# A kernel of three stages on one core: loads and copies of the first pair reordered, the last stage's interleaving rewritten, one VectorE turn split in two

## The chip, the cores and the metric

One core of a Trainium2 chip. The time is that of one execution in microseconds of device time, the median of three runs. A profile of one execution comes with it.

## The reference

Eight samples of 64 rows of width 512 (f32) pass three layers, each added to its input. 

```python
x = x + xattn(layernorm(x), ctx, ctx)   # 1 head: softmax(q k^T / sqrt(512)) v over 1601 context rows
x = x + attn(layernorm(x))              # 16 heads of 32, 64 rows: per head
#   q, k normalised per head; resonance = sigmoid((q k^T - 0.29514) * 15)
#   modulation = resonance * gate_q[:, None] * gate_k[None, :];  out = (modulation @ v) @ Wo + bo
x = x + ffn(layernorm(x))
#   sel = argmax(x @ gate_w.T) of 8 experts, rw = sigmoid(max);  xs = x * rw
#   out = ((xs @ w_up[sel].T) * silu(xs @ w_gate[sel].T)) @ w_down[sel].T
```

## The kernel before, in words

**Pairs.** The eight samples are worked on as four pairs (128 rows each, `p` = 0 to 3). A pair first has its cross attention: *scores* against 1601 keys in 13 units (`score(p, u)`; four units for each of three chunks of 512 keys and one for the last 65), then *sums* (the numerators are turned, `turn_numerators`, copied by ScalarE or VectorE, `move_numerators`, and multiplied with the context, `weigh`). The self attention of pair p-1, its norms and its choice of experts (`attention(p - 1, step)`, step names as in `STEPS`) are laid between the units of pair p by hand. Pairs 1 and 2 are one hardware loop, pair 3 is written out.

**Keys.** Scores need the context with its width on the partitions. For pair 0 some chunks are turned by TensorE (`FIRST.turns`) and copied out of PSUM by ScalarE and VectorE (`move_keys`). All others are loaded into `FF_sb` in pieces of 512 B (`load_split`) and turned in blocks of 32x32 by VectorE (`turn_split(p, ch, c)`, line 874, read at `CT_sb<-FF_sb`). Part 2 of pair p's split load (the third chunk, turned as `turn_split(p, 2, c)`, c = 0 to 3) can only be issued when `turn_split(p, 1, 3)` has freed its slots. `turn_split(p, 2, 0)` is what score unit 4 waits for, `turn_split(p, 2, 3)` is what unit 7 waits for.

**Queues.** SyncE issues nearly all loads in one fixed order, ScalarE issues the upper halves of pair 1's split loads (`upper_first`). GpSimd issues the gathers and scatters of rows (indirect DMAs: `get`, `put`) and does the powers (`pow`) of the norms.

**The ending.** The self attention of the last pair (`_L` = 3) is interleaved with the expert stage, whose rows lie in tiles: four wide ones (0 to 3) and two narrow ones (4 and 5, in a loop over rounds, here one). A tile f has the steps get (gather), xT (turn the rows), up0 to up3 (gate and up product, each a quarter of the depth), act (ScalarE's tanh, then two VectorE instructions), hT (turn), down (product; VectorE adds it to the rows). One table, `ENDING`, then `LATE`, is walked by every engine in order; an engine does what a step holds for it. So a step's place sets what it waits behind on each engine.

## Time and profile before

| | us |
|---|---|
| median of three runs | 330.53 (329.59 to 330.92) |
| the profiled execution's own time | 324.69 |
| its span, first to last instruction | 323.0 |
| TensorE busy | 294.6 (91%), granted clock 0.975 of full speed |
| VectorE, ScalarE, GpSimd busy | 165.2, 87.9, 79.4 |
| the DMA engines, page's slices | nine tenths or more until about two thirds of the span, 240 GB/s on average |

TensorE is the engine to read first; idle times of the others count only where TensorE waits for them. Times of views are from the span's start.

### The profile page before, as it was taken

How to read it: one execution, taken by the hardware profiler on the slowest of the kernel's cores; microseconds unless marked ns; L12 is line 12 of the kernel's file. 1: busy time of each engine (PE TensorE's matmuls, PEld its weight loads, DVE VectorE, ACT ScalarE, POOL GpSimd, SP SyncE). 2: the span in 40 equal slices, each digit the busy share in tenths (PEclk: the TensorE clock that was granted, in tenths of full speed). 3: DMA queues.
4: the chain of work that ended last, by engine and by line, in shares of the span. 5: the costliest groups of instructions: out<-in, count | busy, mean ns of one | idle time of the engine just before them, and what ended most of it. 6: DMA issues, size and time to landing. Idle time of an engine off the chain costs nothing. (4 is left out here: it accounts for less than half of the span.)

```text
span 323.0 us, 4958 instructions
## 1 busy us (share of the span) xinstructions
PE 294.6 (91%) x1628; PEld 143.3 (44%) x1628; DVE 165.2 (51%) x381; ACT 87.9 (27%) x209; POOL 79.4 (25%) x87
## 2 busy tenths in 40 slices
...
GB/s 238 375 296 286 231 315 318 289 232 275 227 386 200 213 270 223 168 306 386 234 229 338 81 207 380 309 298 360 90 67 179 422 411 225 42 213 78 143 13 36
DMA packets 67541, 77.41 MB, mean 240 GB/s; under 512 B 3220, under 2 KB 46260, under 8 KB 66497
## 3 DMA queue, kind: packets, MB, share of 16 engines
...
HBM read 74.00 MB, written 3.67 MB: 240 GB/s over the span
## 5 line engine op out<-in xcount | busy, mean ns | idle before, releaser
L874 DVE STREAM_TRANSPOSE CT_sb<-FF_sb 128x1024 f32<-128x1024 f32 (+1 forms) x56 | 50.7, 952 | 22.0 <-DMA FF_sb<-ctx 20.8
L1385 PE MATMUL ST<-CTX_sb,PR_sb 128*64 128x512 f32 (+1 forms) x208 | 48.2, 600 | 1.1 <-ACT PR_sb L361 1.1
L1347 PE MATMUL SC<-CT_sb,QC_sb 128*64 128x512 f32 x112 | 29.8, 650 | 4.9 <-DVE CT_sb L874 4.9
L1230 PE MATMUL A<-AW_sb,normT_sb 128*128 128x512 f32 x64 | 29.5, 604 | 0.1
L1385 PEld LDWEIGHTS ST<-CTX_sb,PR_sb 128*64 128x64 f32 (+1 forms) x208 | 13.9, 136 | 23.2 <-issue 22.3
L1230 PEld LDWEIGHTS A<-AW_sb,normT_sb 128*128 128x128 f32 x64 | 11.5, 189 | 15.7 <-issue 11.9
L1253 PE MATMUL A<-AW_sb,WQK_sb 128*128 128x256 f32 x64 | 15.9, 412 | 1.5 <-DMA WQK_sb<-wq 1.5
L546 POOL TENSOR_TENSOR rn_sb<-ss_sb,nhalf_sb 128x16 f32<-128x16 f32 x4 | 11.7, 2917 | 22.3 <-DVE ss_sb L948 22.3
L575 POOL TENSOR_TENSOR sq_sb<-AW_sb,rowv_sb 128x512 f32<-128x512 f32 x4 | 5.1, 1273 | 45.9 <-DMA AW_sb<-awk 35.2
L1347 PEld LDWEIGHTS SC<-CT_sb,QC_sb 128*64 128x64 f32 x112 | 7.3, 144 | 20.2 <-issue 11.0
L1230 PE MATMUL A<-AO_sb,rawT_sb 128*128 128x512 f32 x32 | 14.8, 605 | 1.2 <-DVE rawT_sb L987 1.2
L1327 PE MATMUL SC<-CT_sb,QC_sb 128*64 128x256 f32 x112 | 15.7, 418 | 0.0
L1253 PEld LDWEIGHTS A<-AW_sb,WQK_sb 128*128 128x128 f32 x64 | 13.1, 208 | 3.9 <-DMA WQK_sb<-wq 1.8
L1230 PE MATMUL A<-WV_sb,rawT_sb 128*128 128x512 f32 x32 | 14.7, 602 | 0.0
L693 ACT COPY QC_sb<-QK_sb 32x128 f32 (+1 forms) x48 | 14.2, 296 | 1.1
L1286 PE MATMUL A<-AO_sb,WQK_sb 128*128 128x128 f32 (+1 forms) x64 | 14.5, 382 | 0.0
L714 ACT COPY rawT_sb<-A 128x512 f32<-128x512 f32 x4 | 2.3, 586 | 42.8 <-PE A L1223 34.3
L549 POOL TENSOR_TENSOR rn_sb<-ss_sb,nhalf_sb 128x16 f32<-128x16 f32 x4 | 11.6, 2903 | 6.8 <-DVE ss_sb L955 6.8
L540 POOL TENSOR_TENSOR rstd_sb<-rstd_sb,halves_sb 128x3 f32<-128x3 f32 x4 | 3.5, 877 | 39.2 <-DVE rstd_sb L933 39.2
L558 POOL TENSOR_TENSOR rstd_sb<-rstd_sb,nhalf_sb 128x1 f32<-128x1 f32 x4 | 2.2, 562 | 39.5 <-DVE rstd_sb L995 39.5
L701 ACT ACTIVATE PR_sb<-SC,mx_sb 128x512 f32<-128x512 f32 x12 | 8.1, 684 | 12.9 <-DVE mx_sb L898 12.9
L889 DVE TENSOR_REDUCE mx_sb<-SC 128x1 f32<-128x512 f32 x12 | 8.2, 681 | 6.4 <-PE SC L1327 6.3
...
## 6 DMA issues: line engine op xcount, KB each, us to landing
...
FF_sb<-ctx SPq DMA_DIRECT2D x48, 256.0 KB, 6.9
...
FF_sb<-ctx ACTq DMA_DIRECT2D x8, 256.0 KB, 12.1
...
```

The source lines that it names most:

```text
L546: g.tensor_tensor(rn[:, 0:HEADS], ss[:, 0:HEADS], nhalf[:, 0:HEADS], ALU.pow).then_inc(s["powq"], 1)
L549: g.tensor_tensor(rn[:, HEADS:], ss[:, HEADS:], nhalf[:, HEADS:], ALU.pow).then_inc(s["powk"], 1)
L693: a.copy(qcurP[m * Q:(m + 1) * Q, j, :], qk[j * Q:(j + 1) * Q, m, bass.ds(p * P, P)]).then_inc(s["qcurP_made"], 1)
L701: a.activation(prow[:, keys], chunk_scores[c], ACT.Exp, bias=mx[:, NCH + 2:NCH + 3], scale=scale, accum_out=esum[:, c:c + 1]).then_inc(s[" ...
L874: v.transpose(ring[:, c, :, to:to + n * Q].rearrange("p k (b r) -> p k b r", r=Q), split[:, :, at:at + n, c * Q:(c + 1) * Q]).then_inc(s[" ...
L889: link(v.tensor_reduce(mx[:, c:c + 1], chunk_scores[c], AX.X, ALU.max))
L1230: last = t_.matmul(bank, left[:, c, :], right[:, c, :], start=(c == 0), stop=(c == DC - 1))
L1253: last = t_.matmul(AB[m % 2][:, 0:2 * P], wq[:, c, m * P:(m + 1) * P], xnT[:, c, 2 * P * half:2 * P * (half + 1)], start=(c == 0), stop=(c ...
L1286: last = t_.matmul(AB[m % 2][:, n], wkT[:, c, m * P:(m + 1) * P], qpT[:, c, n], start=(c == 0), stop=(c == DC - 1))
L1327: last = t_.matmul(SC[q, at:at + GT * P], queries(p, own)[:, i, q], ring[:, i, k, at:at + GT * P], start=(i == 0), stop=(i == DC - 1))
L1347: last = t_.matmul(SC[q, ch * D:(ch + 1) * D], queries(p, own)[:, c, q], ring[:, c, k, :], start=(c == 0), stop=(c == DC - 1))
L1385: last = t_.matmul(ST[q, :], probs[0:w, t, q], ctxb[0:w, k, t, :], start=(t == 0), stop=(t == KT - 1))
```

## The change

Seven edits: (1) SyncE loads `awq`, `awk` and `wv` later in the first pair; (2) ScalarE copies its last turned keys and a bias row before it issues split loads; (3) VectorE turns pair 1's second chunk ahead of a copy of numerators and of two sums; (4) `turn_split(p, 2, 3)` is done as two halves, by sample, around the normalising of the rows; (5) the tables `ENDING` and `LATE` are reordered, with three wide tiles instead of two stored late; (6) VectorE's five counting instructions stand after `choose(_L)`; (7) the count of stores is taken per queue signal.

```diff
-ENDING = (... (0, "xT"), (_L, "on"), (1, "xT"), (_L, "y"), (0, "up0"), (0, "up1"), (0, "up2"), (0, "up3"),
...
+ENDING = ((0, "get"), (1, "get"), (_L, "sum"), (0, "xT"), (_L, "on"), (_L, "y"), (0, "up0"), (0, "up1"), (0, "up2"), (0, "up3"),
+          (_L, "stats"), (_L, "norm"), (2, "get"), (3, "get"), (_L, "a2"), (0, "act"), (1, "xT"), (_L, "q"), (_L, "graw"), (0, "hT"),
+          (_L, "k"), (_L, "fold"), (_L, "v"), (_L, "kT"), (_L, "turn"), (1, "up0"), (1, "up1"), (_L, "align0"), (_L, "align1"),
+          (0, "down"), (_L, "bd"), (_L, "gT"), (_L, "col"), (2, "xT"), (_L, "o"), (1, "up2"), (_L, "hnorm"), (_L, "h"), (1, "up3"),
+          (_L, "route"), (2, "up0"), (2, "up1"), (_L, "rank"), (2, "up2"))
+LATE = ((1, "act"), (2, "up3"), (1, "hT"), (3, "xT"), (2, "act"), (1, "down"), (3, "up0"), (2, "hT"), (3, "up1"), (3, "up2"),
+        (2, "down"), (3, "up3"), (3, "act"), (3, "hT"), (3, "down"))
-LATE_WIDE = (2, 3)
+LATE_WIDE = (1, 2, 3)
...
             sp.wait_ge(s["qp_made"], 2 * DC)
-            load_weight(awq, "awq", "aq_in")
-            load_weight(awk, "awk", "ak_in")
             load_chunk(0, 1)
             sp.wait_ge(s["keysT_made"], split_turned(0, FIRST.keys(1, 3)))
             load_split(sp, 1, 0, LOWER)
-            load_weight(wv, "wv", "wv_in")
+            load_weight(awq, "awq", "aq_in")
+            load_weight(awk, "awk", "ak_in")
             sp.wait_ge(s["keysT_made"], split_turned(0, FIRST.keys(0, 3)))
             load_split(sp, 1, 1, LOWER)
+            load_weight(wv, "wv", "wv_in")
             load_weight(awv, "awv", "av_in")
...
-            for turn in FIRST.turns[2:6]:
+            for turn in FIRST.turns[2:5]:
+                move_keys(act, a.copy, 0, 0, turn)
+            act.wait_ge(s["c_made"], 1)
+            a.copy(crow, AB[1][:, :]).then_inc(s["c_moved"], 1)
+            for turn in FIRST.turns[5:]:
                 move_keys(act, a.copy, 0, 0, turn)
             upper_first(0, FIRST.keys(1, 3), 0)
-            move_keys(act, a.copy, 0, 0, FIRST.turns[6])
-            act.wait_ge(s["c_made"], 1)
-            a.copy(crow, AB[1][:, :]).then_inc(s["c_moved"], 1)
-            upper_first(0, FIRST.keys(0, 3), 1)
             act.wait_ge(s["c_made"], 2)
             a.copy(call[:], AB[1][:, 0:PAIRS + E]).then_inc(s["c_moved"], 1)
+            upper_first(0, FIRST.keys(0, 3), 1)
...
-            gate_sums(0, 2)
-            move_numerators(dve, v.tensor_copy, 0, 1)
             for c in range(DC):
                 turn_split(1, 1, c)
-            gate_sums(2, 4)
+            move_numerators(dve, v.tensor_copy, 0, 1)
+            gate_sums(0, 4)
             move_numerators(dve, v.tensor_copy, 0, 3)
             gate_sums(4, 2 * DC)
...
-                turn_split(p, 2, 3)
-                chain("norm", "a2")
+                turn_split(p, 2, 3, (slice(0, 1),))
+                chain("norm")
+                turn_split(p, 2, 3, (slice(1, 2),))
+                chain("a2")
```

SyncE at the start of the program, each row a group of loads (`AW_sb`, `WV_sb`, `AO_sb` hold the self attention's and the value weights, `CTX_sb` a chunk of context, `FF_sb` split loads). Before:

```order
L370 DMA FF_sb<-ctx 32x8x128 x8
L411 DMA AW_sb<-awq 128x4x512
L411 DMA AW_sb<-awk 128x4x512
L380 DMA CTX_sb<-ctx 128x4x512 x2
L370 DMA FF_sb<-ctx 32x16x128 x4
L411 DMA WV_sb<-wv 128x4x512
L370 DMA FF_sb<-ctx 32x8x128 x4
L411 DMA AW_sb<-awv 128x4x512
L411 DMA AO_sb<-awo 128x4x512
L370 DMA FF_sb<-ctx 32x16x128 x8
```

The same place now:

```order
L373 DMA FF_sb<-ctx 32x8x128 x8
L383 DMA CTX_sb<-ctx 128x4x512 x2
L373 DMA FF_sb<-ctx 32x16x128 x4
L414 DMA AW_sb<-awq 128x4x512
L414 DMA AW_sb<-awk 128x4x512
L373 DMA FF_sb<-ctx 32x8x128 x4
L414 DMA WV_sb<-wv 128x4x512
L414 DMA AW_sb<-awv 128x4x512
L414 DMA AO_sb<-awo 128x4x512
L373 DMA FF_sb<-ctx 32x16x128 x8
```

The two loads of `awq` and `awk` moved behind the first four split loads of pair 1, and `wv` behind the next four. What stands ahead of the last row, the eight split loads of pair 1's part 2, is the same set.

VectorE in the ending, from the scaling of the last pair's alignments (`res_sb<-A`) on; `WQK_sb<-res_sb` is step bd, `CT_sb<-SC,CT_sb` is the add of (0, "down"), `QK_sb<-QK_sb,SC` is (1, "act"), `rawT_sb<-A,qh_sb` is step col. Before:

```order
L970 TENSOR_TENSOR res_sb<-A,rn_sb 128x512 x2
L981 TENSOR_SCALAR WQK_sb<-res_sb 64x8x64 x4
L1154 SCALAR_TENSOR_TENSOR QK_sb<-QK_sb,SC 128x256
L1155 SCALAR_TENSOR_TENSOR QK_sb<-QK_sb,SC 128x256
L987 TENSOR_TENSOR rawT_sb<-A,qh_sb 128x512
```

The same place now:

```order
L977 TENSOR_TENSOR res_sb<-A,rn_sb 128x512 x2
L1167 TENSOR_TENSOR CT_sb<-SC,CT_sb 128x512
L988 TENSOR_SCALAR WQK_sb<-res_sb 64x8x64 x4
L994 TENSOR_TENSOR rawT_sb<-A,qh_sb 128x512
L1157 COPY QK_sb<-TR 128x512
```

The add of tile 0's product now stands between the two scalings and the four instructions of bd; it stood far ahead of them before. Tile 1's activation has gone from here to the first place of `LATE`.

TensorE at the end of `LATE`; `L1589` (now `L1597`) with `WV_sb` and `WQK_sb` are quarters of tile 3's up product, `L1598` (`L1606`) a turn hT, `L1610` (`L1618`) a down product, `L1572` (`L1580`) two idle matmuls ahead of the last one. Before:

```order
L1598 MATMUL ST<-ident_sb,QK_sb 128x128 x2
L1589 MATMUL SC<-WV_sb,QK_sb 64x512
L1589 MATMUL SC<-WQK_sb,QK_sb 64x512
L1589 MATMUL SC<-WV_sb,QK_sb 64x512
L1589 MATMUL SC<-WQK_sb,QK_sb 64x512
L1610 MATMUL SC<-CTX_sb,QK_sb 64x512 x4
L1598 MATMUL ST<-ident_sb,QK_sb 128x128 x2
L1572 MATMUL SC<-ident_sb 128x128 x2
```

The same place now:

```order
L1606 MATMUL ST<-ident_sb,QK_sb 128x128 x2
L1597 MATMUL SC<-WV_sb,QK_sb 64x512
L1597 MATMUL SC<-WQK_sb,QK_sb 64x512
L1597 MATMUL SC<-WV_sb,QK_sb 64x512
L1597 MATMUL SC<-WQK_sb,QK_sb 64x512
L1618 MATMUL SC<-CTX_sb,QK_sb 64x512 x4
L1597 MATMUL SC<-WV_sb,QK_sb 64x512
L1597 MATMUL SC<-WQK_sb,QK_sb 64x512
L1606 MATMUL ST<-ident_sb,QK_sb 128x128 x2
L1580 MATMUL SC<-ident_sb 128x128 x2
```

Tile 2's down product stood between tile 3's last up quarter and its turn; now the quarter stands directly ahead of the turn.

## Rows read from the trace of the kernel before

**Rows 1.** Busy time by stretch (x instructions): PE, PEld, DVE, ACT, POOL; clock, DMA, GB/s
```profile
80.00:100.00 20.00, 14.43 (x41) 4.57 (x42) 9.28 (x19) 1.17 (x2) 4.22 (x6) 0.83 1.10 298
```

**Rows 2.** TensorE's waits: tile, line, releaser; us in total, times, longest
```profile
PE SC L1347 <- DVE CT_sb L874: 4.9, 1, 4.9
...
PE A L1223 <- DVE a_sb L936: 2.1, 4, 0.7
PE A L1437 <- issue: 1.7, 2, 1.4
PE SC L1327 <- ACT CT_sb L351: 1.5, 1, 1.5
...
PE SC L1589 <- DMA CTX_sb<-wdn: 1.3, 1, 1.3
PE A L1230 <- DVE rawT_sb L987: 1.2, 4, 0.6
...
PE TR L1223 <- DMA CT_sb<-rows,idxg_wide_sb: 1.0, 2, 0.6
PE A L1564 <- DVE CT_sb L1036: 1.0, 1, 1.0
PE A L1223 <- DVE XR_sb L992: 0.6, 1, 0.6
```

**Rows 3.** Timeline, pair 1's wait: start, us, instructions, idle before and releaser
```profile
90.51 5.15 PE L1347 MATMUL SC<-CT_sb,QC_sb 128*64 128x512 f32 x12 [4.90 <-DVE CT_sb L874]
...
89.21 3.50 DVE L874 STREAM_TRANSPOSE CT_sb<-FF_sb 128x1024 f32<-128x1024 f32 x3 [11.51 <-DMA FF_sb<-ctx]
```

**Rows 4.** SyncE's issues from 70 us; DMA issues 82 to 83.2 us, median to landing
```profile
70.25 12.51 SPq L370 DMA_DIRECT2D FF_sb<-ctx  x8
...
FF_sb<-ctx SPq DMA_DIRECT2D x1, 256.0 KB, 7.9
```

**Rows 5.** Two stretches, columns as in group 1
```profile
57.00:62.00 5.00, 5.00 (x35) 3.20 (x32) 2.91 (x8) 2.24 (x8) 1.34 (x2) 0.93 1.23 291
79.00:84.00 5.00, 5.00 (x17) 2.05 (x16) 0.00 (x0) 0.59 (x1) 3.06 (x4) 1.00 1.24 217
```

**Rows 6.** TensorE's timeline, 49 to 58 us
```profile
49.82 1.03 PE L1327 MATMUL SC<-CT_sb,QK_sb 128*64 128x256 f32 x8
...
54.82 3.37 PE L1327 MATMUL SC<-CT_sb,QC_sb 128*64 128x256 f32 x16
```

**Rows 7.** VectorE and GpSimd around pair 2's norm
```profile
147.41 1.24 DVE L874 STREAM_TRANSPOSE CT_sb<-FF_sb 128x1024 f32<-128x1024 f32 x1
148.57 0.51 DVE L936 TENSOR_SCALAR a_sb<-x_sb,mv_sb,rstd_sb 128x512 f32<-128x512 f32 x1
...
147.57 0.87 POOL L540 TENSOR_TENSOR rstd_sb<-rstd_sb,halves_sb 128x3 f32<-128x3 f32 x1 [8.12 <-DVE rstd_sb L933]
```

**Rows 8.** ScalarE's copy of step on; VectorE and GpSimd around the last pair's a2
```profile
247.18 0.59 ACT L711 COPY rawT_sb<-A 128x512 f32<-128x512 f32 x1 [0.75 <-PE A L1223]
...
256.95 2.67 DVE L943 TENSOR_SCALAR normT_sb<-rawT_sb,vec_sb 128x128 f32<-128x128 f32 x4 [1.30 <-ACT rawT_sb L714]
...
257.73 1.28 POOL L543 TENSOR_TENSOR x_sb<-x_sb,rowv_sb 128x512 f32<-128x512 f32 x1
```

**Rows 9.** A down product, its add, step bd
```profile
287.49 1.94 PE L1610 MATMUL SC<-CTX_sb,QK_sb 128*64 128x512 f32 x8
...
272.07 0.69 DVE L1159 TENSOR_TENSOR CT_sb<-SC,CT_sb 128x512 f32<-128x512 f32 x1 [3.52 <-PE SC L1610]
...
278.30 1.78 DVE L981 TENSOR_SCALAR WQK_sb<-res_sb 64x512 f32<-64x512 f32 x4
```

**Rows 10.** One of the counting instructions; one tile's activation, ScalarE then VectorE
```profile
293.42 0.16 DVE L1173 TENSOR_REDUCE cnt_sb<-cnt_sb 128x1 f32<-128x8 f32 x1
...
308.44 0.38 ACT L818 ACTIVATE QK_sb<-TR 128x256 f32<-128x256 f32 x1 [3.34 <-PE TR L1589]
...
308.95 0.42 DVE L1154 SCALAR_TENSOR_TENSOR QK_sb<-QK_sb,TR 128x256 f32<-128x256 f32 x1 [4.33 <-ACT QK_sb L818]
```

More of the change, by code:

```diff
@@ L87 @@
 _B, _L = PAIRS - 2, PAIRS - 1
-ENDING = ((0, "get"), (1, "get"), (_L, "sum"), (0, "xT"), (_L, "on"), (1, "xT"), (_L, "y"), (0, "up0"), (0, "up1"), (0, "up2"), (0, "up3"),
-          (_L, "stats"), (_L, "norm"), (2, "get"), (3, "get"), (_L, "a2"), (1, "up0"), (0, "act"), (_L, "q"), (_L, "graw"), (0, "hT"),
-          (_L, "k"), (_L, "fold"), (_L, "v"), (0, "down"), (2, "xT"), (_L, "kT"), (_L, "turn"), (1, "up1"), (1, "up2"),
-          (_L, "align0"), (_L, "align1"), (1, "up3"), (2, "up0"), (_L, "bd"), (_L, "gT"), (1, "act"), (_L, "col"), (3, "xT"),
-          (_L, "o"), (1, "hT"), (_L, "hnorm"), (_L, "h"), (1, "down"), (_L, "route"), (2, "up1"), (2, "up2"), (_L, "rank"), (2, "up3"))
-LATE = ((2, "act"), (3, "up0"), (3, "up1"), (2, "hT"), (3, "up2"), (3, "up3"), (3, "act"), (2, "down"), (3, "hT"), (3, "down"))
+ENDING = ((0, "get"), (1, "get"), (_L, "sum"), (0, "xT"), (_L, "on"), (_L, "y"), (0, "up0"), (0, "up1"), (0, "up2"), (0, "up3"),
[5 more added lines that the diff above has]
+        (2, "down"), (3, "up3"), (3, "act"), (3, "hT"), (3, "down"))
 FFN_STEPS = ("get", "xT", "up0", "up1", "up2", "up3", "act", "hT", "down")
-LATE_WIDE = (2, 3)
+LATE_WIDE = (1, 2, 3)
 XT_BY_ACT = (3, 4, 5)
@@ L262, in x_bank, with stored @@
             return A1 if f == NT - 1 else TR[0]
-        def stored(r):
-            return 16 * ((NW - len(LATE_WIDE)) // 2 + (len(LATE_WIDE) + NN) // 2 * (r + 1))
+        def stored(i, r):
+            wide = sum(f % 2 == i for f in range(NW) if f not in LATE_WIDE)
+            late = sum(f % 2 == i for f in LATE_WIDE + tuple(range(NW, NT)))
+            return 16 * (wide + late * (r + 1))
         def tile_number(f, r):
@@ L646, in _ @@
                 for i in range(2):
-                    pool.wait_ge(s_stored[i], stored(r))
+                    pool.wait_ge(s_stored[i], stored(i, r))
                 settle(pool)
@@ L866, in _, with turn_split @@
                     v.tensor_scalar(xn[:, t, :], xall[:, t, :], mv[:, t, 0:1], rstd[:, t:t + 1], ALU.subtract, ALU.mult).then_inc(s["xn_made"], 1)
-            def turn_split(p, ch, c):
+            def turn_split(p, ch, c, ks=(slice(0, 2),)):
                 part, at, n = {0: (1, 2 * BLOCKS, BLOCKS), 1: (0, 0, 2 * BLOCKS), 2: (2, 0, 2 * BLOCKS), LOW: (3, 2 * BLOCKS, BLOCKS)}[ch]
@@ L873, in turn_split @@
                 slot_free(dve, p, ch, c)
-                v.transpose(ring[:, c, :, to:to + n * Q].rearrange("p k (b r) -> p k b r", r=Q),
-                            split[:, :, at:at + n, c * Q:(c + 1) * Q]).then_inc(s["keysT_made"], 1)
+                for k in ks:
+                    last = v.transpose(ring[:, c, k, to:to + n * Q].rearrange("p k (b r) -> p k b r", r=Q),
+                                       split[:, k, at:at + n, c * Q:(c + 1) * Q])
+                if ks[-1].stop == 2:
+                    last.then_inc(s["keysT_made"], 1)
             def first_queries():
@@ L1171, in _, with find_rows @@
             link, n = linker("round_chain", 0)
+            def find_rows(link):
+                link(v.tensor_reduce(tok[:, 2, :], token_bank.rearrange("p (i f) -> p f i", i=PAIRS), AX.X, ALU.add))
+                v.tensor_scalar(idxg[:], tok[:, 2, :], -1.0, 0.0, ALU.add, ALU.max).then_inc(s["idxg_made"], 1)
+            dve.wait_ge(s["slot_made"], PAIRS)
+            choose(_L)
             link(v.tensor_tensor(cnt[:, 2:2 + E], A1[:, E:2 * E], filled[:], ALU.add))
```

7 lines of the change are left out of this document (1 added, 6 removed).

## The prediction

> **What bounds the kernel now.** I read the busy table and then TensorE's waits. TensorE is busy for 294.6 of 323.0 us, so a change of order can only win or lose what TensorE idles. Its waits with a releaser [rows 2] hold one large entry, 4.9 us in pair 1, and a dozen small ones. The large one comes in scores unit 4. The timeline shows TensorE starting at 90.51 behind VectorE's turns, and these starting at 89.21 after 11.51 us of waiting for a split load [rows 3]. So a DMA ends that wait: the eight loads of part 2 are issued from 70.25 on for 12.51 us, and the last lands 7.9 us after an issue near 82.5 [rows 4]. The stretch around it has a granted clock of 0.83 [rows 1], so some of the work behind the wait ran at 1.2 instead of 2.4 GHz: 12 matmuls took 5.15 us, of which full clock would have needed half, 2.6. The wait thus costs 4.9 + 2.6 = 7.5 us and is the only prize of that size. From there to the ending TensorE has no wait over 1.4 us.
>
> **The loads and copies of the first pair (edits 1 to 3).** The old ScalarE order issues four split loads between two copies of keys, and TensorE waits 1.5 us for the second copy [rows 2]. The clock falls behind it: 16 matmuls take 3.37 us where 8 took 1.03 [rows 6], 1.3 us more. Both go. But that is 2.8 us ahead of a wait that a DMA ends, so TensorE only comes to unit 4 earlier and waits longer. What counts is when part 2 has landed, and ahead of it the queue holds the same seven 1 MB loads and the same sixteen split loads (half of them ScalarE's), only in another order. Was the DMA free in between? From 79 to 84 us it is busy at 1.24 with 217 GB/s, from 57 to 62 at 1.23 with 291 [rows 5]. In both it moves pieces of 512 B; in the second, two queues give them at once. Nothing is free there, so the bound for gain is small unless the order itself is cheaper. Edit 3 lets VectorE free the slots some 4 us earlier, so SyncE issues part 2 from 66 instead of 70 us; but even the last of the eight lands 7.9 us after its issue [rows 4], behind what is already queued. An earlier issue into a full queue buys nothing.
> For a loss: SyncE's four loads for pair 1's first part now run without ScalarE's four beside them, since ScalarE issues later. 1 MB at 217 instead of 291 GB/s takes 4.8 instead of 3.6 us: +1.2. The low bound is a gain of all 7.5 us, the high bound a loss of 2 (that term and a short gap at 45 us, when only two loads are queued). The rows speak for a small loss, and I take +0.5.
> The Trainium skill (DMA: Bandwidth & Descriptors, Issuing engines are not separate DMA queues) says that queues of several engines share the same 16 DMA engines and that issuing from several saves only issue time. By that page the term of 1.2 would be nothing, and the total change +2.4. The rates of the two stretches differ by a third, so the rows speak against it here.
>
> **The split turn (edit 4), three times.** GpSimd's power runs from 147.57 for 0.87 us and ends at 148.44; VectorE's turn begins at 147.41 and the normalising follows at 148.57 [rows 7]. With half a turn ahead (estimate 0.65) it could start at about 148.48: 0.1 us won. The second half then ends some 0.7 us after the normalising, about 0.1 us after TensorE has turned the rows and wants unit 7. The two cancel: 0 for all three pairs, within 0.3 either way. Its cover is unit 7's own 1 us, which hides the earlier arrival of what `q` needs. If that cover were gone it could win 0.3 in all.
>
> **The ending (edits 5 to 7).** All matmuls are the same, so I compare TensorE's waits. I followed the table step by step with the durations of the old trace.
> Waits that go or shrink [rows 2]: tile 1's turn for its gather 0.6; its up0 for a weight load 1.3; align0 0.3 (line 1437's shorter one); `o` 0.6, now 0.3; `h` 0.6, now 0; the find_tokens matmuls 1.0, now 0.2 (edit 6 takes five VectorE instructions, 0.2 apart, from ahead of `choose(_L)` [rows 10]). Together 4.4, of which 0.5 stays.
> Waits that come:
> (a) `y` stands right behind `on`, and ScalarE's copy between them takes 0.6 us [rows 8], with its signals 0.8.
> (b) `q` no longer has up0 of tile 1 ahead of it, only a turn of 0.55. normT's four instructions take 2.67 instead of about 1.1 us, and end their long one with GpSimd's bias add, 257.73 + 1.28 = 259.01 [rows 8]. GpSimd's order is unchanged, so this stays. TensorE waits 0.7 for the first and 1.1 inside the product: 1.8. The weight wait of 1.3 had hidden it.
> (c) `(0, "down")` on VectorE stands between align1 and bd. TensorE does that product after align1: 1.9 us, then VectorE adds for 0.69, then bd takes 1.78 [rows 9]. TensorE has only gT (0.6) before `col`, which needs bd. So 0.69 + 1.78 - 0.6 and the signals: 2.0, where it had next to none.
> (d) `(1, "act")` follows the five counting and two index instructions on VectorE, some 1.3 us at 0.2 each [rows 10], and takes 0.9 itself; TensorE has only one up quarter (0.9) in that time ahead of tile 1's turn hT: 1.0 by the steps.
> (e) `(3, "up3")` stands directly ahead of hT of tile 3. An activation runs from 308.44 (ScalarE) over 308.95 (VectorE's first) to the end of a second VectorE instruction like the first, near 309.8 [rows 10]: 1.4. It had been hidden by tile 2's down product of 1.9 us.
> Sum: 0.5 + 0.8 + 1.8 + 2.0 + 1.0 + 1.4 = 7.5 against 4.4, +3.1. Followed by the same steps, the old table gives 5.2 where the rows have 4.4: my steps overstate short waits. Like for like it is +2.3, unrounded +2.4.
> The third late store adds a scatter of about 1 us on GpSimd before the last ones, in a stretch where TensorE works for 10 us: 0; with that cover gone it would cost 1. The earlier gathers of tiles 4 and 5 start 3 us earlier and save nothing, since TensorE did not wait for them.
>
> **The sum.** 0.5 + 0 + 2.4 = +2.9 on a profiled 324.69. That execution lies 5.8 us below the median of the runs; I add the change to the median: 330.53 + 2.9 = 333.4.
>
> **The rivals.**
> *The new waits cost clock too.* Behind the wait of 1.5 us at line 1327 the clock fell, with one-column matmuls following it; behind that of 1.4 at line 1437 it did not (the page's slices show full clock there). The new wait at `col` is 2.0. A fall costs 1.3 by [rows 6], two of them 2.6; with part 2 landing 1 us later: 335 to 337. Chance 0.14.
> *The first pair pays (the other side).* If part 2 lands earlier, because the pieces mix better with the weights or the queue had unseen gaps, every us is won, and the clock cost goes with the wait. It decides from 4.1 us on (2.4 + 1.65). The full prize gives 330.53 + 2.4 - 7.5 = 325.4, half of it 329. For it: the split loads of pair 1's first part now stand ahead of two weights, so VectorE can free the slots sooner. Against: the DMA is full in both stretches. Chance 0.21.
> *The waits I name are covered, and nothing happens.* If VectorE's add is not late and the counted waits are half as long, the ending is even: 329.5 to 332. Chance 0.15.
> *The forecast*, 332.2 to 335: chance 0.50.
>
> **How the numbers follow.** 0.5% is 1.65 us, about what a measurement can tell from no change. Slower: forecast and first rival, 0.64. Same: 0.15 and a little from the prize rival, 0.16. Faster 0.20. The range leaves out about one in ten on each side: the full prize below, two falls of the clock and a late load above: 327.5 to 336.3. The likeliest case's own range is 332.2 to 335.
>
> **What would show it.** TensorE's wait at scores unit 4 of pair 1: 6 to 8 us, still with VectorE waiting for `FF_sb`, ending at 90 to 91. No wait at line 1327's successor. a_sb waits (4 of them) about 0.5 each as before. A wait of 2 us before `col` for VectorE's bd, of 1.0 before tile 1's hT, 1.4 before tile 3's, 1.8 around `q`. Wrong would be: unit 4 starting before 88, or bd not behind the add.

## The result, and the profile after

The changed kernel takes 334.55 us (median of 20 executions, 329.70 to 337.72), the kernel before 329.52 (20 executions, 320.71 to 336.92). The measured ratio is 1.028, 95% interval 1.020 to 1.035; it leaves out the executions that lie over 1.5% above the quickest of their kernel, and five profiles below, marked *, are of such executions. Over all executions the medians differ by 5.0 us, 1.5%. With the later runs added, 70 executions of the kernel before have a mean of 328.9 us and 26 of the changed one 334.1: +5.2 us, with a standard error of 0.7 (scatters of 3.8 and 2.6). The change makes the kernel slower; I had forecast +2.9.

The profiled execution has a span of 330.4 us instead of 323.0. TensorE's waits after, with the columns of [rows 2]:

```profile
PE TR L1364 <- ACT PR_sb L704: 3.9, 1, 3.9
PE A L1231 <- DVE a_sb L943: 3.8, 4, 1.9
...
PE A L1445 <- issue: 2.8, 2, 2.5
...
PE ST L1606 <- DVE QK_sb L1163: 2.3, 2, 1.5
PE A L1460 <- DVE WQK_sb L988: 1.9, 1, 1.9
PE A L1238 <- DVE normT_sb L950: 1.3, 2, 0.7
...
PE A L1238 <- ACT rawT_sb L714: 0.7, 1, 0.7
...
PE A L1572 <- DVE CT_sb L1043: 0.2, 1, 0.2
```

The wait of 4.9 us in scores unit 4 is gone. The last five rows are the ending's, as foretold: hT of tiles 1 and 3, col behind bd, q, y, and the rest of the find_tokens wait. The first row was not foretold; the wait that I had expected to grow was the one in unit 4. The new one is followed back through four engines in the timeline of the changed kernel (columns as in [rows 3]):

```profile
61.89 1.26 POOL L578 TENSOR_TENSOR sq_sb<-AW_sb,rowv_sb 128x512 f32<-128x512 f32 x1 [47.53 <-DMA AW_sb<-awk]
63.11 1.26 POOL L578 TENSOR_TENSOR kh_sb<-AW_sb,rowv_sb 128x512 f32<-128x512 f32 x1
64.31 0.18 POOL L532 COPY ccur_sb<-call_sb 128x1 f32<-128x1 f32 x1
...
64.60 0.16 DVE L904 TENSOR_TENSOR mx_sb<-mx_sb,ccur_sb 128x1 f32<-128x1 f32 x1 [7.20 <-POOL ccur_sb L532]
...
65.04 0.69 ACT L704 ACTIVATE PR_sb<-SC,mx_sb 128x512 f32<-128x512 f32 x1 [9.41 <-DVE mx_sb L905]
...
65.87 1.51 PE L1364 MATMUL TR<-ident_sb,PR_sb 128*128 128x128 f32 x8 [3.90 <-ACT PR_sb L704]
...
68.36 4.62 DVE L879 STREAM_TRANSPOSE CT_sb<-FF_sb 128x1024 f32<-128x1024 f32 x4 [3.08 <-DMA FF_sb<-ctx]
...
73.09 9.15 SPq L373 DMA_DIRECT2D FF_sb<-ctx  x8
...
89.09 3.50 DVE L879 STREAM_TRANSPOSE CT_sb<-FF_sb 128x1024 f32<-128x1024 f32 x3 [5.34 <-DMA FF_sb<-ctx]
...
90.58 3.65 PE L1355 MATMUL SC<-CT_sb,QC_sb 128*64 128x512 f32 x16
96.12 0.66 PE L1231 MATMUL A<-ident_sb,a_sb 128*128 128x128 f32 x4 [1.88 <-DVE a_sb L943]
96.81 1.25 PE L1355 MATMUL SC<-CT_sb,QC_sb 128*64 128x512 f32 x4
97.99 5.18 PE L1238 MATMUL A<-AW_sb,normT_sb 128*128 128x512 f32 x8
```

GpSimd does its first two gate products (`sq_sb`, `kh_sb`), which need `awk`, and only then copies pair 0's column into `ccur_sb`. Edit 1 moved `awk` back, so the copy came at 64.31 us instead of 58.30. VectorE's shift (`mx_sb<-mx_sb,ccur_sb`, the largest score adjusted by that column), ScalarE's exponentials and TensorE's turns of the numerators followed, one after another. VectorE's turns of pair 1's second chunk stand behind that shift too. In this profile they waited 3.08 us longer, for their split loads, and began at 68.36 (before 65.5). Part 2 was issued from 73.09 on (before 70.25), not from 66 as I had said. Still it landed at 89.1, as before. The row at 90.58 begins with unit 3, and unit 4 follows at about 91.5, a us after VectorE had made it possible; so the new wait and the old one swapped places. From VectorE's first turn of part 2 to TensorE's turns of `a_sb` it is 7.03 us here and 7.07 before: that chain is VectorE's, and the clock at which TensorE does units 4 to 6 is hidden under it. What was not hidden is behind it. In both kernels q begins at 97.99, and its eight matmuls took 5.18 us, with the granted clock down from 97.5 to 101. Before:

```profile
97.99 3.70 PE L1230 MATMUL A<-AW_sb,normT_sb 128*128 128x512 f32 x8
```

The busy table by stretch, columns as in [rows 1]:

```profile
80.00:100.00 20.00, 18.08 (x69) 6.29 (x66) 12.02 (x26) 2.81 (x7) 10.02 (x8) 0.94 1.09 293
79.00:84.00 5.00, 5.00 (x27) 1.73 (x27) 3.07 (x7) 2.01 (x8) 3.94 (x4) 1.00 1.24 202
45.00:50.00 5.00, 5.00 (x31) 2.32 (x28) 4.31 (x6) 1.25 (x3) 0.00 (x0) 1.00 0.82 202
```

The last row is the gap in the queue that I had put into the upper bound: a DMA share of 0.82. It is not shown to be a mark of the change: the same stretch has a share of 1.16 in a second profile of the changed kernel and 1.13 in one with edits 1 to 3 alone. Before, it had:

```profile
45.00:50.00 5.00, 5.00 (x32) 2.44 (x30) 3.10 (x5) 0.59 (x1) 0.42 (x1) 1.00 1.01 382
```

**Where the 7.4 us of span lie.** The alignments (TensorE, line 1437, now 1445) mark the three pairs. Before they start at 111.92, 164.78 and 219.24 us:

```profile
113.39 1.90 PE L1445 MATMUL A<-WQK_sb,rawT_sb 128*64 128x256 f32 x16
167.14 1.95 PE L1445 MATMUL A<-WQK_sb,rawT_sb 128*64 128x256 f32 x16 [0.27 <-issue]
222.87 2.73 PE L1445 MATMUL A<-WQK_sb,rawT_sb 128*64 128x256 f32 x16 [2.53 <-issue]
...
251.35 0.66 PE L1231 MATMUL TR<-ident_sb,CT_sb 128*128 128x128 f32 x4 [0.56 <-DMA CT_sb<-rows,idxg_wide_sb]
```

The last row, the turn of tile 0, begins the ending; before it starts at 246.01. So the first pair has +1.5 (all of it the slow q), pairs 2 and 3 +2.2, from there to the ending +1.7, and the ending +2.1 (79.1 instead of 77.0). Whether each of these belongs to the change is what the runs had to tell.

### The profile page after: what moved, and what is told of

The parts are those of the page before. It is cut to its first block, busy times and chain, and to the rows that moved or that the text cites. A ratio compares the mean times of both kernels' runs of the same rounds, so it can differ in the third digit from the quotient of the medians.

```text
span 330.4 us, 4965 instructions
## 1 busy us (share of the span) xinstructions
PE 298.9 (90%) x1628; PEld 145.5 (44%) x1628; DVE 166.0 (50%) x384; ACT 87.4 (26%) x209; POOL 79.4 (24%) x87
## 4 chain that ended last, share of the span: by engine, by line
PE 54%; DMA 17%; DVE 15%; issue 5%; SPq 5%; POOL 1%; ACT 1%; ACTq 0%; DVEq 0%; POOLq 0%
PE A L1238 15%; DMA FF_sb<-ctx 12%; DVE CT_sb L879 6%; PE A L1261 5%; SPq L373 4%; PE SC L1335 4%; PE SC L1597 3%; PE SC L1618 3%; PE TR L1238 3%; PE SC L1355 3%; PE A L1294 3%; PE A L1445 2%; PE A L1231 2%; DMA WQK_sb<-wq 2%; DMA CT_sb<-rows,idxg_wide_sb 1%
## 5 line engine op out<-in xcount | busy, mean ns | idle before, releaser
L879 DVE STREAM_TRANSPOSE CT_sb<-FF_sb 128x512 f32<-128x512 f32 (+1 forms) x59 | 51.2, 912 | 21.0 <-DMA FF_sb<-ctx 19.8
L1393 PE MATMUL ST<-CTX_sb,PR_sb 128*64 128x512 f32 (+1 forms) x208 | 50.6, 625 | 2.4 <-ACT PR_sb L364 2.4
L1238 PE MATMUL A<-AW_sb,normT_sb 128*128 128x512 f32 x64 | 31.3, 631 | 1.3 <-DVE normT_sb L950 1.3
L1355 PE MATMUL SC<-CT_sb,QC_sb 128*64 128x512 f32 x112 | 27.4, 606 | 0.1
L1261 PE MATMUL A<-AW_sb,WQK_sb 128*128 128x256 f32 x64 | 17.3, 438 | 1.2 <-DMA WQK_sb<-wq 1.2
L1261 PEld LDWEIGHTS A<-AW_sb,WQK_sb 128*128 128x128 f32 x64 | 14.2, 225 | 4.1 <-DMA WQK_sb<-wq 1.6
L1335 PE MATMUL SC<-CT_sb,QC_sb 128*64 128x256 f32 x112 | 14.6, 395 | 0.0
L552 POOL TENSOR_TENSOR rn_sb<-ss_sb,nhalf_sb 128x16 f32<-128x16 f32 x4 | 11.6, 2909 | 6.7 <-DVE ss_sb L962 6.7
L1355 PEld LDWEIGHTS SC<-CT_sb,QC_sb 128*64 128x64 f32 x112 | 7.0, 136 | 13.9 <-issue 10.6
L1364 PE MATMUL TR<-ident_sb,PR_sb 128*128 128x128 f32 (+1 forms) x52 | 8.5, 287 | 3.9 <-ACT PR_sb L704 3.9
L1294 PEld LDWEIGHTS A<-AO_sb,WQK_sb 128*128 128x128 f32 x64 | 9.6, 191 | 3.8
## 6 DMA issues: line engine op xcount, KB each, us to landing
CTX_sb<-ctx SPq DMA_DIRECT2D x24, 1024.0 KB, 11.6
```

Source lines behind the costliest of these rows:

```text
L552: g.tensor_tensor(rn[:, HEADS:], ss[:, HEADS:], nhalf[:, HEADS:], ALU.pow).then_inc(s["powk"], 1)
L879: last = v.transpose(ring[:, c, k, to:to + n * Q].rearrange("p k (b r) -> p k b r", r=Q), split[:, k, at:at + n, c * Q:(c + 1) * Q])
L1238: last = t_.matmul(bank, left[:, c, :], right[:, c, :], start=(c == 0), stop=(c == DC - 1))
L1261: last = t_.matmul(AB[m % 2][:, 0:2 * P], wq[:, c, m * P:(m + 1) * P], xnT[:, c, 2 * P * half:2 * P * (half + 1)], start=(c == 0), stop=(c ...
L1294: last = t_.matmul(AB[m % 2][:, n], wkT[:, c, m * P:(m + 1) * P], qpT[:, c, n], start=(c == 0), stop=(c == DC - 1))
L1335: last = t_.matmul(SC[q, at:at + GT * P], queries(p, own)[:, i, q], ring[:, i, k, at:at + GT * P], start=(i == 0), stop=(i == DC - 1))
```

## The experiments

Fifteen runs followed, of twelve new programs and three repeated ones, each with a profile and six executions beside eleven of the kernel before. This table has the marks of every profile: when GpSimd starts on `awk`, when VectorE begins to turn pair 1's second chunk and its part 2, the alignments of pair 1, from these to the alignments of pair 3, and the ending from tile 0's turn to the end of the span (us). The mark * is that of the result's section.

| kernel | awk | chunk 2 | part 2 | align 1 | pairs 2+3 | ending | ratio, 95% interval |
|---|---|---|---|---|---|---|---|
| before | 49.6 | 65.5 | 89.2 | 111.9 | 107.3 | 77.0 | |
| before_again | 46.1 | 61.3 | 86.4 | 109.1 | 109.0 | 77.0 | 0.999 (0.990 to 1.007) |
| after | 61.9 | 68.4 | 89.1 | 113.4 | 109.5 | 79.1 | 1.028 (1.020 to 1.035) |
| after_again | 67.9 | 71.2 | 93.3 | 117.0 | 108.7 | 79.1 | 1.016 (1.007 to 1.026) |
| ending_only | 48.4 | 64.1 | 87.1 | 110.1 | 110.0 | 80.7 | 1.017 (1.010 to 1.025) |
| first_pair_only | 68.1 | 71.4 | 91.1 | 115.4 | 108.1 | 77.2 | 1.016 (1.010 to 1.022) |
| split_turn_only | 47.8 | 65.4 | 92.0 | 114.7 | 109.7 | 77.1 | 1.010 (1.003 to 1.018) |
| loads_moved* | 74.2 | 80.8 | 98.8 | 122.4 | 107.9 | 77.4 | 1.012 (1.007 to 1.017) |
| loads_unmoved | 49.5 | 66.7 | 93.6 | 116.4 | 109.0 | 77.1 | 1.008 (1.000 to 1.016) |
| bias_first* | 66.0 | 68.3 | 91.1 | 116.5 | 109.5 | 80.4 | 1.020 (1.009 to 1.030) |
| first_pair_bias* | 69.0 | 70.2 | 95.0 | 117.7 | 108.8 | 77.3 | 1.007 (0.997 to 1.017) |
| weights_later | 46.9 | 65.8 | 83.7 | 111.8 | 110.3 | 77.2 | 0.993 (0.984 to 1.002) |
| two_queues | 45.4 | 61.7 | 87.2 | 110.3 | 108.5 | 77.4 | 0.999 (0.991 to 1.006) |
| awo_later* | 52.2 | 70.4 | 92.3 | 118.3 | 110.7 | 77.3 | 0.990 (0.979 to 1.000) |
| ending_mended* | 52.1 | 71.5 | 98.7 | 121.4 | 110.2 | 75.9 | 1.001 (0.992 to 1.010) |
| awo_and_table | 49.3 | 65.4 | 86.1 | 111.5 | 108.8 | 76.4 | 0.987 (0.979 to 0.996) |
| awo_and_table_2 | 53.7 | 70.6 | 92.9 | 118.3 | 108.1 | 76.4 | 1.013 (1.007 to 1.019) |

**The same program twice.** before_again and after_again change nothing.

> The kernel before once more, under another name. It tells how far executions of one program differ, stage by stage. Theory A (the program repeats but for what the DMA delivers): from TensorE's first work of the ending (line 1223's turn for tile 0) to the end of the span it takes 77.0 us as before, within 0.1 but for falls of the clock; the landing of part 2 in pair 1 is somewhere from 87 to 92 us, and the waits in pairs 2 and 3 sum to 4 to 6.5 us. Theory B (before is a quick program by its edits): waits of pairs 2 and 3 near 4.1 us again.

> The changed kernel once more. Theory A (what the profiles so far show by stage): TensorE comes to the alignments of pair 1 (line 1437's successor) 24.3 to 25.4 us after VectorE's first turn of part 2, where kernels with the old load order need 22.7, since the clock falls at q; the ending from line 1223's turn for tile 0 on takes 79.1 us, or 80.6 with a fall of the clock behind the wait at col, instead of 77.0. Exponentials of pair 0 wait for GpSimd's ccur again. Theory B (the fall at q was chance): 22.7 us, the same as before. The landing of part 2 may be anywhere from 87 to 92 us.

The ending repeats to 0.02 us in both, 77.0 and 79.1; all ten profiles with the old table lie between 77.0 and 77.4. The first pair does not repeat: part 2 lands from 86.4 to 92.0 in the four unmarked profiles that have the first pair and its loads as before (before, before_again, ending_only, split_turn_only). Pairs 2 and 3 take 107.9 to 110.7 us in all other profiles; before's 107.3 was the quickest, so its difference of 2.2 to after is mostly the one profile. The fall of the clock near 220 us came in before_again too: its way from the alignments of pair 3 to the ending took 28.4 us, like after's 28.5 and unlike before's 26.8. So 1.7 of the 7.4 us are no mark of the change either. Of after_again's theory A, the ending and the wait for `ccur` held and the first part did not: align 1 is 23.7 us behind part 2, less than the 24.3 to 25.4 foretold, and the clock did not fall at q; it had fallen earlier, during a wait of 11.6 us for the exponentials.

**One part alone.** ending_only has edits 5 to 7, first_pair_only edits 1 to 3, split_turn_only edit 4.

> The kernel before with edits 5 to 7 alone (the tables, the three late tiles, the five counting instructions). Theory A (each edit's waits add, and nothing else): everything up to the ending stands as before, and from TensorE's `on` to the end of the span it takes 2.1 us more than before, by the waits at `y` 0.7, `q` 1.3, `col` 1.9, hT of tile 1 0.9 and hT of tile 3 1.5; ratio about 1.006, span about 325. Theory B (the granted clock also falls in the ending, behind the wait of 1.9): 1.5 more, ratio 1.011. Theory C (the loss between the profiles is chiefly in executions, not in edits): ratio within 1.003 of 1, whatever the waits in the profile.

> The kernel before with edits 1 to 3 alone. Theory A: part 2 of pair 1 lands at 89 us as before; GpSimd waits for `awk` until some 62 us, then does two gate products and only then the copy of pair 0's column (ccur), so that VectorE, ScalarE's exponentials and TensorE's numerator turns are late: a new wait of 3.9 us at about 66 us, which takes the place of the one of 4.9 at unit 4; both kernels are level again by 98 us. Then the clock falls behind the a_sb wait of 1.9 us in pair 1 and `q` takes 1.5 us longer; ratio 1.005. Theory B (a fall of the clock belongs to an execution and not to the edits): no fall at 98 us here, ratio 1.000. Theory C (edits 1 to 3 also make part 3 of pair 3 land 1.1 us later): the align wait of pair 3 is 2.5 instead of 1.4 us here, ratio 1.010.

> The kernel before with edit 4 alone. Theory A: GpSimd's power becomes what the normalising waits for, 0.4 us on VectorE three times, and TensorE is late by 0.1 to 0.3 us for each pair; 0.3 to 0.8 us in all, ratio 1.001 to 1.003. Theory B (edit 4 delays the signal that frees the last slots, so that the low part of pair 3 is issued and lands later): the align wait of pair 3 grows from 1.4 to about 2.5 us, ratio 1.004 and with a fall of the clock behind it 1.008. Theory C: nothing, ratio 1.000.

ending_only shows the foretold waits, to 0.1 us, and behind the one at col the clock fell (theory B); its ratio of 1.017 is above what either theory gave. Rows from the wait on:

```profile
278.98 1.65 PE L1455 MATMUL A<-WQK_sb,vs_sb 128*32 128x128 f32 x32 [1.89 <-DVE WQK_sb L984]
280.56 1.12 PE L1226 MATMUL TR<-ident_sb,PR_sb 128*128 128x128 f32 x4
281.47 4.29 PE L1233 MATMUL A<-AO_sb,rawT_sb 128*128 128x512 f32 x8
```

In after, the first and last of these took 1.08 and 3.70:

```profile
283.44 1.08 PE L1460 MATMUL A<-WQK_sb,vs_sb 128*32 128x128 f32 x32 [1.89 <-DVE WQK_sb L988]
285.34 3.70 PE L1238 MATMUL A<-AO_sb,rawT_sb 128*128 128x512 f32 x8 [0.23 <-DVE rawT_sb L994]
```

bias_first fell there as well, after and after_again did not. The ending costs 2.1 us, or 3.4 to 3.7 with the fall, which came in two profiles of four. first_pair_only had theory A's wait, but of 11.5 us instead of 3.9, and no fall at q. Its loss behind the landing was that TensorE came to unit 4 at 96.9 us, 5.7 us after VectorE's first turn of part 2, where 1.3 are enough in before. In split_turn_only pairs 2 and 3 took 109.7 us, and 109.4 on average in the four profiles with this edit, against 109.0 in the thirteen without it, which scatter from 107.3 to 110.7. The wait for GpSimd's power is there (the first half of the turn, then the normalising):

```profile
151.24 0.70 DVE L875 STREAM_TRANSPOSE CT_sb<-FF_sb 128x512 f32<-128x512 f32 x1
152.30 0.55 DVE L939 TENSOR_SCALAR a_sb<-x_sb,mv_sb,rstd_sb 128x512 f32<-128x512 f32 x1 [0.36 <-POOL rstd_sb L540]
```

With [rows 7], a_sb came 1.16 us behind the turn's start before and 1.06 here. The 0.1 that I had worked out is right. Its timed ratio of 1.010 is not explained by it. One program timed twice, below, gave 0.987 and then 1.013 with intervals that do not overlap, so the ratio of one run of six executions shows no difference of this size, and no cost of edit 4 is shown.

**Which edit of the first pair.** loads_moved is edit 1 alone, loads_unmoved edits 2 and 3 without it. bias_first (on the changed kernel) and first_pair_bias (edits 1 to 3 alone) take GpSimd's wait away:

```diff
+            pair_bias(0)
             pool.wait_ge(s["rowv_in"], 16)
...
             for n in range(2 * DC):
-                if n == 2:
-                    pair_bias(0)
```

> The changed kernel with GpSimd's copy of pair 0's column (pair_bias(0)) ahead of its waits for `awq` and `awk`. Theory A (that order makes the wait of 3.9 us at 66 us): that wait and the fall of the clock behind it go; TensorE comes to unit 4 of pair 1 near 84 us instead of 91 and waits there for part 2 until 89.1, as was foretold for the change. Since a DMA ends that wait, pair 1 goes on at the same time as in the changed kernel, so the total is within 0.5 us of it: ratio to before as the changed kernel's, 1.02. Theory B (the wait is a real loss): the total falls by 2 to 4 us. Theory C: the long wait moves the clock's falls, and the `q` of pair 1 and the align of pair 3 come out 1.5 us shorter each.

> The kernel before with edit 1 alone (SyncE loads `awq`, `awk` and `wv` later). Theory A (GpSimd's copy of ccur waits behind its gate products for `awk`, and VectorE's shift, which needs ccur, stands ahead of the turns of pair 1's second chunk): these turns start at 68 to 71 us instead of 61 to 65, part 2 is issued from 73 to 76 us on instead of 66 to 70, lands 2 us later on average, and the alignments of pair 1 come near 112 us instead of 108; ratio 1.01. Theory B (edits 2 and 3 make the loss): alignments near 108, ratio 1.00.

> The kernel before with edits 2 and 3 but without edit 1: SyncE loads `awq` and `awk` where it did. Theory A (edit 1 costs in the first pair, by the empty queue at 45 us and by GpSimd's wait for `awk`): no wait for GpSimd's ccur, the DMA moves about 380 GB/s at 45 to 50 us as before instead of 202, pair 1's second chunk is turned from 66 us on instead of 68 to 71, and the total is 0 to 1 us from before. Theory B (edit 2, the later issue by ScalarE, does it): the second chunk is turned from 68 on here too, exponentials start behind ScalarE's issues near 62 us, and the total is 2 us over before, as with edits 1 to 3.

> Edits 1 to 3 with GpSimd's copy of ccur ahead of its waits for the gate weights: first_pair_only without its wait. Theory A (as for loads_moved): no wait of TensorE for the exponentials over 1.5 us, the second chunk's turns are started by the DMA near 68 us, alignments 22.7 us behind the landing of part 2, near 110 to 111; ratio 1.005, and 2 us less than first_pair_only. Theory B (the wait is hidden whenever it occurs): as first_pair_only, alignments from 112 to 114.

Three of these expectations missed in part. bias_first's total is not told apart from the changed kernel's, as theory A said, but TensorE did not come to unit 4 near 84: the copies and turns of the numerators held it until 91.6, and it waited there for only 0.85 us. loads_moved was foretold to begin the turns at 68 to 71 and did at 80.8. first_pair_bias kept a wait of 4.4 us for the exponentials, where theory A allowed 1.5.

In loads_moved the wait is at its largest (timeline of GpSimd, TensorE and SyncE):

```profile
76.67 0.18 POOL L529 COPY ccur_sb<-call_sb 128x1 f32<-128x1 f32 x1
...
78.23 1.97 PE L1356 MATMUL TR<-ident_sb,PR_sb 128*128 128x128 f32 x8 [18.97 <-ACT PR_sb L701]
...
85.56 5.78 SPq L370 DMA_DIRECT2D FF_sb<-ctx  x8
```

So edit 1 makes this wait. GpSimd starts on `awk` at 61.9 to 74.2 us with edit 1 and at 45.4 to 53.7 without, with no overlap, and TensorE's wait for the exponentials is 3.9, 11.6, 11.5 and 19.0 us in the four profiles that have edit 1 and the old place of the copy. With the copy ahead it is 0.9 (bias_first) and 4.4 us (first_pair_bias, where ScalarE's own split loads, which edit 2 put ahead of the exponentials, hold it). In loads_unmoved GpSimd is no matter, and the waits come from edits 2 and 3:

```profile
62.70 3.65 PE L1385 MATMUL ST<-CTX_sb,PR_sb 128*64 128x512 f32 x16 [1.55 <-ACT PR_sb L361]
71.95 5.05 PE L1385 MATMUL ST<-CTX_sb,PR_sb 128*64 128x512 f32 x16 [5.01 <-DVE PR_sb L361]
94.95 4.63 PE L1347 MATMUL SC<-CT_sb,QC_sb 128*64 128x512 f32 x12 [5.30 <-DVE CT_sb L875]
```

The second is edit 3's price: VectorE copies the numerators only behind four turns that wait for their load. Both are ahead of the third, a wait that the DMA ends, so they cost nothing here. But this profile, without edit 1 and GpSimd's wait, reaches align 1 at 116.4 us, later than first_pair_only, because part 2 landed at 93.6.

With `awo` in its old place, the eight profiles in which TensorE still waits 3 us and more in unit 4 reach align 1 from 22.7 to 23.1 us behind the first turn of part 2; the five in which it came too late for that (after, after_again, first_pair_only, loads_moved, bias_first) need 23.6 to 25.3. The reasons differ. In after_again, first_pair_only and loads_moved TensorE came late to unit 4, behind GpSimd's wait. In after and bias_first the clock fell at q, behind a wait of 1.9 and 2.4 us for `a_sb`, and bias_first waited 1.2 at the alignments besides. first_pair_bias, with edits 1 to 3 but not GpSimd's wait, needs 22.7.

What lets the turns of the second chunk begin is not one thing either (before_again, then after_again's shift and turns, then bias_first):

```profile
61.32 4.62 DVE L874 STREAM_TRANSPOSE CT_sb<-FF_sb 128x1024 f32<-128x1024 f32 x4 [1.02 <-DMA FF_sb<-ctx]
...
70.60 0.16 DVE L904 TENSOR_TENSOR mx_sb<-mx_sb,ccur_sb 128x1 f32<-128x1 f32 x1 [14.88 <-POOL ccur_sb L532]
71.20 4.62 DVE L879 STREAM_TRANSPOSE CT_sb<-FF_sb 128x1024 f32<-128x1024 f32 x4
...
68.31 4.62 DVE L878 STREAM_TRANSPOSE CT_sb<-FF_sb 128x1024 f32<-128x1024 f32 x4 [9.59 <-DMA FF_sb<-ctx]
```

GpSimd's wait holds them in after_again, first_pair_only and loads_moved. Without it the split loads do: at 66.7 in loads_unmoved, 68.3 in bias_first, 70.2 in first_pair_bias, and, in the old order, at 61.3, 64.1 and 65.4 in before_again, ending_only and split_turn_only, where VectorE already waited 1.0 to 3.3 us for them.

And the start of part 2's issue does not set when it lands. The loads ahead of it do, the last of which is `awo` (time from issue to landing, before and after):

```profile
AO_sb<-awo SPq DMA_DIRECT2D x1, 1024.0 KB, 15.2
...
AO_sb<-awo SPq DMA_DIRECT2D x1, 1024.0 KB, 16.6
```

Issued at 64.0 and 62.0, it landed at 79.2 and 78.6, and part 2 at 89.1 and 89.0. In all twelve profiles in which part 2 is issued behind `awo` and before this has landed, it lands 9.0 to 10.3 us after `awo`, though its issue began anywhere from 66.1 to 76.3. Only in loads_moved, where it began at 85.6 with `awo` landed at 84.8, is it 13.9.

How large the first pair's share is stays uncertain. Align 1 is at 109.1 to 114.7 us in the four unmarked profiles with the first pair and its loads unchanged (mean 111.4), and at 113.4 to 117.0 in the three unmarked ones with edits 1 to 3 (mean 115.3). That is +3.8 before rounding, with a scatter of 2 to 3 us between executions. Of it, 2.5 lie in the landing of part 2 (means 88.7 and 91.2), which is not told apart from the scatter, and 1.3 behind the landing (22.7 to 23.0 against 23.7 to 24.3), where the two groups do not overlap. Taking GpSimd's wait away gave no clear gain: the intervals of first_pair_bias and bias_first overlap those of first_pair_only and the changed kernel.

**Can part 2 come earlier?** weights_later puts `awv` and `awo` behind part 2's loads, awo_later `awo` alone; two_queues lets ScalarE issue part 2's upper half.

The edit of awo_later, then that of two_queues:

```diff
-            load_weight(awo, "awo", "awo_in")
             split_after(1, NEXT.keys(1, 3), 1, 2)
+            load_weight(awo, "awo", "awo_in")
```

```diff
-            split_after(1, NEXT.keys(1, 3), 1, 2)
+            sp.wait_ge(s["keysT_made"], split_turned(1, NEXT.keys(1, 3)))
+            load_split(sp, 1, 2, LOWER)
...
             next_queries(1, range(DC))
+            act.wait_ge(s["keysT_made"], split_turned(1, NEXT.keys(1, 3)))
+            load_split(act, 1, 2, UPPER)
```

> The kernel before with the loads of `awv` and `awo`, 2 MB, behind the eight split loads of pair 1's part 2 instead of ahead of them. They are first needed at steps v and o of pair 0's attention, 20 us after unit 4. Theory A (the landing of part 2 is set by the bytes ahead of it, and pair 1's wait is a loss of its own): part 2 lands at 84 to 86 us instead of 89, the wait of 4.9 us and the clock's fall at 88 go, and the total falls by 5 to 7 us. Theory B (the DMA bounds the whole first two thirds): part 2 lands earlier just so, but pair 2's part 2 lands when it did, near 142 us, since the same bytes go ahead of it; TensorE waits there, at unit 4 or for a_sb, by what it won, and the total is within 1 us of before. Theory C (nothing was queued behind these two): landing at 89 again.

> The kernel before with the load of `awo` alone (1 MB) behind part 2's split loads; `awv` stays, since weights_later made TensorE wait 3.7 us for it. Theory A (all that follows hangs on the landing of part 2 in pair 1: 22.7 us later come the alignments, 53.5 later the same landing of pair 2): part 2 lands 15 to 16 us after its first issue instead of 18 to 19, no wait at 108 us, and the total falls by 2 to 3 us, ratio 0.992 to 0.994. Theory B (the DMA gives back in pair 2 what it lends here): the landing of pair 2's part 2 is more than 55 us behind that of pair 1, total as before. Theory C: awo was not in the way, landing 18 to 19 us after the issue.

> The kernel before with the eight split loads of pair 1's part 2 shared: SyncE issues the four lower ones, ScalarE the four upper ones, behind its copies of the next queries. Theory A (two queues move pieces of 512 B faster, 291 GB/s against 217 in the rows of before): the eight loads land 15 to 16 us after the first issue instead of 18 to 19, part 2 near 86 us, and the total falls by up to 2 us. Theory B (several queues share the same DMA engines, as the Trainium skill says in DMA: Bandwidth & Descriptors, Issuing engines are not separate DMA queues): the rate at 79 to 84 us stays near 217 GB/s, the landing at 89, and ScalarE's issues delay its work for step on by up to 5 us, which the wait for part 2 hides: total within 1 us of before. Theory C: ScalarE's issues are so slow that TensorE waits for it longer than for part 2, +2 us.

weights_later moved the landing to 83.7 us, and the wait in unit 4 went. But the next split load of the same pair, which step align waits for by way of VectorE, came no earlier (TensorE, then VectorE; before, VectorE turned it from 107.8 on):

```profile
90.80 0.94 PE L1223 MATMUL A<-ident_sb,a_sb 128*128 128x128 f32 x4 [2.44 <-DVE a_sb L936]
111.78 3.47 PE L1437 MATMUL A<-WQK_sb,rawT_sb 128*64 128x256 f32 x16 [3.70 <-issue]
...
107.74 2.49 DVE L874 STREAM_TRANSPOSE CT_sb<-FF_sb 128x512 f32<-128x512 f32 x4 [3.90 <-DMA FF_sb<-ctx]
```

Theory B holds, a pair sooner than it said: the queue takes back within pair 1 what it gave. My reason in awo_later's expectation, that `awv` made that wait, was wrong; it shows the same wait, 3.1 us, with `awv` in its old place. In two_queues part 2 was issued from 66.37 on and landed at 87.18, 20.8 us later. The issues took 6.15 us instead of 12.51, and part 2 landed no sooner after the first of them than before (19.0). The rate from 79 to 84 us was 275 GB/s, with the 1 MB loads of the next chunks, issued from 73.00 on, among the pieces.

**The mended table.** ending_mended has edits 5 to 7 with three places changed; awo_and_table and awo_and_table_2 are the same program, this table and awo_later's order.

```diff
-          (0, "down"), (_L, "bd"), (_L, "gT"), (_L, "col"),
+          (_L, "bd"), (0, "down"), (_L, "gT"), (_L, "col"),
...
-LATE = ((1, "act"), (2, "up3"), (1, "hT"), (3, "xT"), (2, "act"), (1, "down"),
+LATE = ((1, "act"), (2, "up3"), (3, "xT"), (1, "hT"), (2, "act"), (1, "down"),
...
-        (2, "down"), (3, "up3"), (3, "act"), (3, "hT"), (3, "down"))
+        (3, "up3"), (3, "act"), (2, "down"), (3, "hT"), (3, "down"))
```

> The kernel before with edits 5 to 7, in a table mended at three places: (0, down) stands behind step bd instead of ahead of it, the turn xT of tile 3 ahead of tile 1's turn hT, and tile 2's down product between tile 3's activation and its turn hT again. Theory A (the ending's loss is the three waits of col, 1.9, hT of tile 1, 0.9, and hT of tile 3, 1.5): col's wait and hT 3's go, hT 1's falls to 0.3, and the ending from line 1223's turn for tile 0 on takes 75.2 us, where before has 77.0 and the new table 79.1. No fall of the clock near 280 us, which ending_only had behind the wait of col. Theory B (the waits move on: bd's add now delays VectorE's col instruction, or the later product delays something else): 76.5 to 77.5 us. Theory C: 79 us, the waits have another cause.

> The kernel before with awo_later's load order and the mended table of ending_mended. Theory A (the two gains are in different stages and add): alignments 22.7 us behind the landing of part 2, the ending from line 1223's turn for tile 0 on 75.9 us as in ending_mended, where before has 77.0; 3 to 4 us less than before, ratio 0.988 to 0.991. Theory B (the table's gain of 1.1 us is taken back by a fall of the clock in the ending, as in ending_only): ratio 0.994.

> awo_and_table once more, since its interval still touches no change. Theory A (it is the better kernel): ratio of 0.985 to 0.995 again, the ending from line 1223's turn for tile 0 on 75.9 us without a fall of the clock ahead of its last 5 us. Theory B (its six runs were lucky): ratio within 0.003 of 1.

The three waits were 1.89, 0.85 and 1.48 us in after; in ending_mended they are 0.19, 0.27 and none (col, hT of tile 1, hT of tile 3):

```profile
288.88 1.08 PE L1455 MATMUL A<-WQK_sb,vs_sb 128*32 128x128 f32 x32 [0.19 <-DVE WQK_sb L984]
...
303.46 0.41 PE L1601 MATMUL ST<-ident_sb,QK_sb 128*128 128x128 f32 x2 [0.27 <-DVE QK_sb L1158]
...
311.87 0.44 PE L1601 MATMUL ST<-ident_sb,QK_sb 128*128 128x128 f32 x2
```

The ending takes 75.9 to 76.4 us in all three profiles, 0.6 to 1.1 less than before and 2.7 to 3.2 less than the new table, with no fall of the clock ahead of its last 5 us. In the total this drowns: the two timings of the same program gave 0.987 (0.979 to 0.996) and 1.013 (1.007 to 1.019), so an interval from six executions is narrower than what they differ by from run to run. No kernel here is shown to beat the one before.

## Why the prediction was half right

**Direction.** Slower was right, and the time of 334.55 lies in the range, but the forecast was 0.9% and the medians say 1.5%, the means of all executions 1.6%, the ratio 2.8%. The likeliest case was too small.

**The first pair, +0.5: the step that failed.** The term measured +3.8 by the means above, of which 1.3 behind the landing are clear of the scatter. "Edit 3 lets VectorE free the slots some 4 us earlier, so SyncE issues part 2 from 66 instead of 70 us" was wrong in sign: 73, 76 and 76 us in the three unmarked profiles. Two waits were missing from it. VectorE's turns need the second chunk's split loads, which in the old order were landing just then, so there were no 4 us to gain; and they stand behind the shift. I had followed the moved loads through SyncE's and ScalarE's queues and not to those who wait for them: GpSimd waits for `awk` with the copy of `ccur` queued behind, and on that copy hang VectorE, ScalarE and TensorE. So "TensorE only comes to unit 4 earlier" failed as well. It came at 91.5, 98.0 and 96.9, where before it stood ready at 85.6 and waited. No case of the prediction held this. That an earlier issue buys nothing was right, and a later one cost nothing either until `awo` had landed.

**The wait is worth 7.5 us.** Also wrong. The slow matmuls behind the wait (2.6 us by my halving, 2.4 by the 16 that took 3.65 in after) were hidden: a_sb comes 7.0 us after part 2's first turn at either clock. And the 4.9 were not to be had by the orders tried: weights_later took the wait away and met the next split load. A slip in the reading: the last of the eight is issued from 81.2 to 82.8, and its 7.9 us count from 81.2.

**Two queues, +1.2.** Not borne out as a rule: whatever made the rates of the two stretches differ, a second queue did not bring part 2 sooner; SyncE's issues took half the time and part 2 landed 20.8 instead of 19.0 us after the first. The Trainium skill (DMA: Bandwidth & Descriptors, Issuing engines are not separate DMA queues) says that issuing from several engines saves only the time of issuing. This trace agrees with it, and not with my reading.

**The split turn, 0.** By the rows right (0.1 us earlier into a_sb); any effect on the total is below what these runs tell.

**The ending, +2.4.** Measured 2.1 in waits. By terms: y 0.7 (0.8), q 1.3 (1.8), col 1.9 (2.0), hT of tile 1 0.9 (1.0), hT of tile 3 1.5 (1.4), o 0.2 (0.3), find_tokens 0.2 (0.2). That is the mechanism as foretold. ending_mended, which moved three steps, each aimed at one wait, shows the causes of col and the two hT; q, which I had at 1.8, stays.

**The clock rival, 0.14.** Its mechanism came: behind the wait at col in two of the four profiles with the new table, 1.3 to 1.6 us. A term of about half of that belonged into the sum.

Together: 2.1 in the ending, near 0.7 for its clock, and the first pair with 2 to 4 us are in keeping with the 5.2 that the executions show; the first pair's share is the uncertain one. What stays open is whether edits 1 to 3 make part 2 land later at all: the 2.5 us lie within the scatter, and loads_unmoved landed late without edit 1. The direction came true by the ending, which was priced rightly; the first pair's term had the right sign for reasons that did not occur, and that is luck.
